# Layer 3 of a four-layer kernel: the expert units move from four bursts into the slots of the recurrence

## The reference

```python
# s: delta rule in chunks of 32 tokens, 4 heads of 32 channels
def step(S, inp):
    q_i, k_i, u_i, w_i = inp
    attn = jnp.where(causal, q_i @ k_i.T, 0.0)
    u_adj = u_i - w_i @ S
    o_i = q_i @ S + attn @ u_adj
    return (S + k_i.T @ u_adj, o_i)
# then s = rmsnorm(gated mix of o_i, three FIR filters and v) @ Wo.T
# f: mixture of experts, 8 experts, 2 per token, capacity 1280 tokens each
hid = einsum('ech,ehf->ecf', inp, W_in);  a, g = split(hid, 2)
out_e = einsum('ecf,efh->ech', gelu(a) * g, W_out)   # then gathered back and weighted
```

## Time and profile before

| what | value |
|---|---|
| the profiled execution's own time | 3312.5 us |
| its span, first to last instruction | 3310.7 us |
| mean granted TensorE clock, share of 2.4 GHz | 0.882 |
| TensorE matmul busy | 2952.2 us, 89% |
| VectorE, ScalarE, GpSimd busy | 56%, 40%, 43% |
| first burst to the end | from 2617 us on |

### The profile page before, as it was taken

How to read it: one execution, slowest core, us unless ns; L and a number is a source line. 1 busy time by engine, 2 the same in 40 slices (tenths; PEclk the granted TensorE clock), 3 DMA queues, 4 the chain that set the end, 5 groups by cost and what they waited for, 6 DMA issues and landing times.

```text
span 3310.7 us, 38793 instructions
## 1 busy us (share of the span) xinstructions
PE 2952.2 (89%) x13864; PEld 1823.9 (55%) x13864; DVE 1841.8 (56%) x3075; ACT 1314.4 (40%) x3221; POOL 1429.1 (43%) x1348
## 2 busy tenths in 40 slices
PE   7896799999999998799999999999789788888876
PEld 3564355555555555355555554444478666666765
DVE  6868577677777766465655554444433534343313
ACT  4453433443443343345555555444412342413201
POOL 3324366676676776267777775000013200101144
PEclk8997899999999999799999999998777775857666
DMA  5451100000000000600000000221022111111111
GB/s 183 151 181 53 50 1 1 1 1 1 1 1 1 1 1 1 145 17 14 1 1 1 1 1 20 74 74 64 30 64 87 43 28 37 31 40 39 34 39 45
DMA packets 160928, 128.88 MB, mean 39 GB/s; under 512 B 97688, under 2 KB 136864, under 8 KB 160224
## 3 DMA queue, kind: packets, MB, share of 16 engines
q1 hardware_dynamic: 148832, 90.13, 9.7%
q0 software_dynamic: 11904, 36.27, 3.4%
HBM read 105.70 MB, written 38.47 MB: 44 GB/s over the span
## 4 chain that ended last, share of the span: by engine, by line
PE 49%; DVE 4%; ACT 3%; issue 2%; another core or an unknown queue 1%; SPq 0%; POOL 0%; DMA 0%; DVEq 0%; ACTq 0%
PE bank L63 44%; PE bank L2051 4%; DVE work L3178 1%; DVE work L3180 1%; SPq L3198 0%; DVE work L3137 0%; ACT L3105 0%; PE bank L2749 0%; DVE weights_even L3137 0%; DVE work L1984 0%; DVE work L3294 0%; POOL weights_odd L2814 0%; PE bank L2904 0%; ACT work L3106 0%
## 5 line engine op out<-in xcount | busy, mean ns | idle before, releaser
L63 PE MATMUL bank<-work 64*128 64x256 f32 (+5 forms) x4384 | 654.3, 365 | 28.1 <-DVE work L3294 7.9
L1491 POOL TENSOR_TENSOR work<-work 128x512 f32<-128x512 f32 x384 | 494.9, 1289 | 320.4 <-DVE work L1483 303.4
L63 PEld LDWEIGHTS bank<-work 64*128 64x128 f32 (+4 forms) x4384 | 468.3, 185 | 260.2 <-issue 137.3
L2039 POOL TENSOR_SCALAR work<-work 128x256 f32<-128x256 f32 x512 | 465.0, 926 | 240.9 <-DVE work L2030 240.8
L63 PE MATMUL bank<-weights_odd,normed_channels 128*128 128x512 f32 (+3 forms) x1152 | 527.9, 566 | 22.4 <-DVE work L1483 15.4
L63 PE MATMUL bank<-work,weights_even 128*32 128x128 f32 (+4 forms) x1136 | 344.9, 482 | 50.0 <-DVE work L1010 15.7
L2024 ACT ACTIVATE work<-bank,work 128x256 f32<-128x256 f32 x512 | 235.9, 473 | 195.0 <-DVE work L2010 190.9
L1483 DVE TENSOR_TENSOR work<-bank,work 128x512 f32<-128x512 f32 x360 | 245.5, 686 | 110.0 <-PE bank L63 106.5
L63 PEld LDWEIGHTS bank<-weights_odd,normed_channels 128*128 128x128 f32 x1152 | 186.6, 199 | 161.5 <-issue 83.1
L63 PEld LDWEIGHTS bank<-work,weights_even 128*32 128x32 f32 (+4 forms) x1136 | 162.2, 193 | 194.4 <-issue 136.4
L2783 POOL TENSOR_TENSOR weights_odd<-weights_odd 128x512 f32<-128x512 f32 x40 | 50.7, 1267 | 491.6 <-ACT weights_odd L2778 491.6
(11 more groups left out here) (307 smaller groups left out, 4535.4 us busy)
## 6 DMA issues: line engine op xcount, KB each, us to landing
work<-gate_rows_L SPq DMA_DIRECT2D x64, 256.0 KB, 3.1
filter_matrices<-in_L_filters SPq DMA_DIRECT2D x24, 512.0 KB, 8.1
work<-filter_matrices SPq DMA_DIRECT2D x16, 768.0 KB, 4.2
expert_rows_in<-in_zeros SPq DMA_DIRECT2D x8, 640.0 KB, 11.3
weights_odd<-expert_rows_in SPq DMA_DIRECT2D x40, 128.0 KB
expert_rows_out<-weights_odd SPq DMA_DIRECT2D x40, 128.0 KB
weights_even<-expert_rows_in SPq DMA_DIRECT2D x20, 128.0 KB
expert_rows_out<-weights_even SPq DMA_DIRECT2D x20, 128.0 KB
```

What stands on the lines that cost most here:

```text
L63: return pe.matmul(out, lhsT, rhs, start=first, stop=last, skip_group_check=True)
L1491: gp.tensor_tensor(self.sum_of(p), self.sum_of(p), self.product_of(p), ALU.add).then_inc(s["l1_add"], 1)
L2039: gp.tensor_scalar(p[:, c], p[:, c], self.sums(n, half, i), None, ALU.mult).then_inc(s["l2_p"], 1)
```

## The change

The bursts go. Quarter 0 gets 14 units, quarters 1 and 2 get 13 each, quarter 3 none. Unit n of a quarter has its place in slot 5 + 3n, its up one slot later and its down in the slot where the next unit is placed. The first seven units of a quarter use banks 2 (a, y) and 7 (x, g), which uw leaves free and the heads take later; the others use banks 0 and 1, after the front is done. The waits follow: heads 0 and 1 wait for unit 6's y and g copies, the next front for the last unit. GpSimd takes all 40 in one loop. On SyncE the grams, results, weights and loads are issued slot by slot, and `sync_inverses` stands at slot 37. The mix loads the table for Ln and Exp right after Square.

```diff
+L3_UNITS_OF = (14, 13, 13, 0)
+L3_UNIT_SLOT, L3_UNIT_STEP, L3_FIRST_SET = 5, 3, 7
+def unit_due(q, slot, lag):
+    n = event(slot, L3_UNIT_SLOT, L3_UNIT_STEP, lag, L3_UNITS_OF[q])
+    return None if n is None else sum(L3_UNITS_OF[:q]) + n
-        self.b_stage, self.b_x, self.b_y, self.b_a, self.b_g = b[7], b[4], b[3], (b[0], b[2]), (b[1], b[7])
+        self.b_stage, self.b_ya, self.b_xg = b[7], (b[2], b[0]), (b[7], b[1])
-    def tensor_burst(self, pe, on, quarter):
...
+    def tensor_units(self, pe, on, quarter, slot):
+        if (n := unit_due(quarter, slot, 3)) is not None:
+            self.tensor_down(pe, on, n)
+        if (n := unit_due(quarter, slot, 0)) is not None:
+            self.tensor_place(pe, on, quarter, n)
+        if (n := unit_due(quarter, slot, 1)) is not None:
+            self.tensor_up(pe, on, n)
...
+            elif L3_UNITS_OF[quarter] > 0:
+                self.moe_done(on, "moe_act", MOE_ACT, (("y", "second")[n], last_unit(quarter, 0)))
...
             a.activation(x, cols(self.sum, g), ACT.Square).then_inc(done, 1)
+            a.preload_act_table_set(EXP_AND_LN)
             self.done(on, "l3_mix_mm", MIX_MM, g, "mean")
...
         for quarter in range(QUARTERS):
-            self.tensor_burst(pe, on, quarter)
             for slot in range(L3_PERIOD + self.TAIL * (quarter == QUARTERS - 1)):
...
                 elif (g := self.join_due(slot, 1)) is not None:
                     self.tensor_join(pe, on, g)
+                self.tensor_units(pe, on, quarter, slot)
...
+        for quarter in range(QUARTERS - 1):
+            self.sync_triangles(sp, on, quarter + 1)
+            for slot in range(L3_PERIOD):
+                for n, step in self.front_steps(quarter, slot):
+                    if step >= 6 and (g := self.front_of(n, 1)) is not None:
+                        self.sync_gram(sp, on, g, step - 6)
+                if (n := unit_due(quarter, slot, 3)) is not None:
+                    self.sync_result(sp, on, n)
+                    e, last = divmod(n + 1, L3_PER_EXPERT)
+                    if last == 0 and e + 1 < EXPERTS:
+                        self.sync_weights(sp, on, e + 1)
+                if (n := unit_due(quarter, slot, 0)) is not None and n + 3 < L3_UNITS:
+                    self.sync_place(sp, on, n + 3)
+                if slot == self.INVERTED:
+                    self.sync_inverses(sp, on, quarter + 1)
+    INVERTED = 37
```

More of the change, by code:

```diff
@@ L2318, with unit_set, last_unit @@
 MIX_DVE = ("gate", "sum", "unit")
-MOE_STEPS = tuple((q, t) for q in range(QUARTERS) for t in range(L3_BURST + 3))
-def unit_due(q, t, lag):
-    return q * L3_BURST + t - lag if 0 <= t - lag < L3_BURST else None
+def unit_due(q, slot, lag):
+    n = event(slot, L3_UNIT_SLOT, L3_UNIT_STEP, lag, L3_UNITS_OF[q])
+    return None if n is None else sum(L3_UNITS_OF[:q]) + n
+def unit_set(n):
+    q = next(q for q in range(QUARTERS) if n < sum(L3_UNITS_OF[:q + 1]))
+    return int(n - sum(L3_UNITS_OF[:q]) >= L3_FIRST_SET)
+def last_unit(q, which):
+    return sum(L3_UNITS_OF[:q]) + (L3_FIRST_SET if which == 0 else L3_UNITS_OF[q]) - 1
 def events(parts):
-    return tuple((what, unit_due(q, t, lag)) for q, t in MOE_STEPS for what, lag in parts if unit_due(q, t, lag) is not None)
+    return tuple((what, unit_due(q, slot, lag)) for q in range(QUARTERS) for slot in range(L3_PERIOD) for what, lag in parts
+                 if unit_due(q, slot, lag) is not None)
 BY_GROUP = lambda what: tuple((what, g) for g in range(GROUPS))
-MOE_MM = BY_GROUP("stage") + events((("x", 0), ("a", 1), ("g", 1), ("y", 3))) + BY_GROUP("join")
-MOE_ACT = BY_GROUP("stage") + events((("x", 0), ("gelu", 1), ("second", 1), ("y", 3))) + BY_GROUP("silu")
+MOE_MM = BY_GROUP("stage") + events((("y", 3), ("x", 0), ("a", 1), ("g", 1))) + BY_GROUP("join")
+MOE_ACT = BY_GROUP("stage") + events((("y", 3), ("x", 0), ("gelu", 1), ("second", 1))) + BY_GROUP("silu")
 MOE_POOL = events((("gated", 1),)) + BY_GROUP("scale")
@@ L3210, in tensor_uw @@
             on.wait_ge(s["l3_sum_act"], 2 * GROUPS)
+            self.moe_done(on, "moe_act", MOE_ACT, ("stage", GROUPS - 1))
         else:
@@ L3510, in scalar @@
                     self.scalar_silu(a, on, g)
+                self.scalar_units(a, on, quarter, slot)
     def vector(self, v, on):
@@ L3571, in gpsimd @@
         next(setup)
-        for quarter in range(QUARTERS):
-            self.gpsimd_burst(gp, on, quarter)
+        for n in range(L3_UNITS):
+            self.gpsimd_gated(gp, on, n)
         for g in range(GROUPS + 2):
```

80 lines of the change are left out of this document (31 added, 49 removed).

## The result

The changed kernel takes 3260.69 us in the median of four runs (3257.80 to 3272.97); the kernel before, beside it, takes 3305.99 (3295.89 to 3312.02). The ratio is 0.9873, with an interval of 0.9836 to 0.9911: 1.3% faster, 45.3 us. The prediction said 3273, faster, with a range from 3220 to 3332.

A forecast was written before the change was run, and what follows sets the result against it. TensorE, busy 89% of the span, was taken as the bound, its clock deciding the sign. Terms -129.8 + 9 + 35 + 40 + 13 - 2.5 + 6 gave about -29 us off 3302.5: 3273 us, range 3220 to 3332.

The forecast's parts named there:

- rival 2: Recurrence clock stays at 0.67 to 0.78 and units pay the half price: +45, 3347 us, slower; chance 0.20 with what lies toward it.
- The recurrence: Slots 4 to 27, 8 units per quarter: four fifths of work at full clock, +35 us, 1.5 per unit.
- The heads: Slots 28 to 36, 3 units per quarter, no idle time to give: net 4.4 us per unit, +40.
- A unit here starts at 5.9: Heads: a unit costs 5.9 us, the half-clock price, before any gain from raising the clock.
- One in two, for some 3.4 us: Heads: one up in two raises the clock for some 3.4 us, saving about 1.5 us per unit.
- Rival 1: Full clock everywhere, heads and mix too: about -142, 3160 us, half the way 3217; chance 0.08 in full or half.
- The mix: Slots 37 to 47, 3, 2 and 2 units: 28.1, 24.2, 24.2 us against 21.4, called +13.
- A Gelu has two slots until its down, 5 us or more: Quarters 0 to 2: Gelu table loads of 1.28 us, some four per period, are covered and cost nothing.
- some 1.5 of the waits stays: Mix, busy 12.4 of 21.4 us before: with units in it, only some 1.5 us of TensorE's waits remain.
- SyncE's queue: Unit results stand behind 32 inverse DMAs from slot 37 on: 2 us of wait per period, +6, bounds 0 and 24.
- Rival 3: SyncE's queue becomes the wait, 8 us per period instead of 2: +18, 3291 us; chance 0.20 together with rival 4.
- Rival 4: Nothing hidden, each unit lengthens its period by 2.84 us: -9, 3293 us; chance 0.20 together with rival 3.

The follow-up runs named there:

- thin units: Changed kernel with each unit's up and down matmuls cut to three of 32 columns, all waits, copies, products and DMAs kept; 3260.15 us in one run.

## Why the prediction was right

**Removal and sign.** The bursts went as a whole and nothing else in their place: -129.8. The clock decided, as said: rival 2, which had the recurrence at 0.78 or below, is excluded by 0.89 to 0.91, and thin units show the half of it that is true: without dense matmuls the clock of two of the three recurrences is 0.64 and 0.66 (0.84 in the third).

**The recurrence, right.** Predicted 78, 79 and 64 us; measured 77.4, 81.0 and 65.9. Per unit 1.6 against 1.5. The clock came as assumed; two smaller misses nearly cancel, by luck: the pauses left are 7.6, 9.6 and 8.4 us where 5, 6.5 and 5 were put, and the busy time is 1.3 to 3.1 us shorter. The timeline of TensorE in the first of them, changed kernel: transposes, gram, up, w and o, all at full clock in the order assumed.

```profile
2685.73 0.38 PE L2748 MATMUL bank<-constants,weights_odd 128*128 128x128 f32 x2
2686.04 1.15 PE L63 MATMUL bank<-work,weights_even 32*128 32x128 f32 x8
2687.62 1.89 PE L63 MATMUL bank<-weights_odd 128*128 128x256 f32 x8
2689.44 1.06 PE L63 MATMUL bank<-work 128*32 128x128 f32 x8
2690.34 1.04 PE L63 MATMUL bank<-work,weights_even 128*32 128x128 f32 x8
```

**The heads, mis-sized by half.** 4.4 us a unit predicted, 2.3 measured (20.5 over nine). The step that failed is "A unit here starts at 5.9", which has the stage begin at half clock. The recurrence hands over its full clock, and the first 10 to 11 us of each heads stage still run at it; the first up there takes 1.97 us each time. After that the clock falls, and "One in two, for some 3.4 us" was near the mark: of the three ups that ran at half clock, the one in the first period (2753.95) was followed by 3 us at full clock, the two others by none. The heads of the first and of the second period in the changed kernel:

```profile
2740.93 1.97 PE L63 MATMUL bank<-weights_odd 128*128 128x256 f32 x8
2742.83 1.15 PE L63 MATMUL bank<-weights_even 32*128 32x128 f32 x8
...
2918.81 3.76 PE L63 MATMUL bank<-weights_odd 128*128 128x256 f32 x8
2922.51 7.76 PE L63 MATMUL bank<-work 32*128 32x128 f32 x32
```

The first up of a stage takes 1.97 us, a later one 3.76, with 32 small records behind it in 7.76. Rival 1, the clock up everywhere, had a third of its way here: 0.73, 0.65 and 0.64 where it wanted 1.00. The Trainium skill, TensorE: Matmul & The Clock Gate, section Why this matters for your kernels, advises to keep TensorE continuously busy for the full clock. The heads of the changed kernel have at most 1.7 us without matmul in 34 and are still at 0.64 to 0.73, so here too the trace agrees only in part.

**The mix, mis-sized the other way.** The step that failed is "A Gelu has two slots until its down, 5 us or more". Between the up and the down of a mix's last unit (of its last two in the first mix) the two slots hold no other matmul, so TensorE waits for the whole of the unit's chain, 3.55 us with the table load and 2.12 without. With it goes "some 1.5 of the waits stays". The units there cost 22.8 us, 3.3 each, against 13 plus 6 for a stall. The clock was better than assumed (0.88), but the time without matmul is 11.2, 8.7 and 8.6 us, where it was 9.0 before and 1.5 were to stay. Most of the old waits were filled, as meant. One of TensorE's waits for VectorE in a mix of the kernel before, and the same matmul in the changed one:

```profile
2789.26 2.07 PE L63 MATMUL bank<-work,weights_odd 128*128 128x512 f32 x2 [2.23 <-DVE work L3378]
```

```profile
2778.60 1.02 PE L63 MATMUL bank<-work,weights_odd 128*128 128x512 f32 x2
```

Of the 9.0 us, 3.0 are left (for Square and the mix's own copy). New ones took their place, 8.2, 5.7 and 5.6 us, all of them for the units' own steps: 5.6, 3.5 and 3.6 for GpSimd's product, the rest for the copies. Table loads are a part of that: without the Gelu's the mixes are 5.5 us shorter, though the three periods only 1, and without the preload 18.6 longer. Thin units, whose three mixes are only 1.6 us shorter, show that it is the unit's chain and not its matmuls; taking two units away (-12) shows the place.

**SyncE's queue, +6 predicted, 0 measured.** TensorE and ScalarE wait for no result. The inverse DMAs' issue (from 2936.78, 15.0 us) ends ahead of the next uw by 10 us, for the longer mix gives it time. Rival 3 did not occur. Rival 4, nothing hidden at 2.84 a unit, would be 3293 us; the recurrence's 1.6 is below it, and thin units show that its sum of parts is wrong in kind: TensorE's price for a unit can't be added without what it does to the clock.

**uw and the last period.** Three uw cost 4.5, where four were put at 9 because each would start at half clock. Only the first did (7.04 us for its first u); the others took 5.42, 3.77 and 3.92, behind mixes whose units had the clock up. With one unit in two slots, where the mixes have no unit, it is 6.9 each time. The last period is 8.6 us shorter, 2.5 of it the preload. The other 6 were not foreseen, and their cause stays open: nothing else is edited there but the start, and TensorE does the same work in 103.1 us in place of 111.3, at a clock of 0.68 in place of 0.63. The period takes 140 to 157 us in eight executions with units in the slots and the joins left alone, and 159.2 and 157.1 in the two with bursts.

From -29 to -54.7 lead the heads (-19.5), uw (-4.5), start and last period (-8.4), the recurrence (+3.2) and mix with SyncE's queue (+3.8). By the medians the change won 45.3 us where 29.5 were forecast. The prediction stood above the median of the runs by 12.3 us, 0.4%, and not by the 15.8 between the two gains, because the kernel before also came out 3.5 us slower than the median it started from. That it stood so close is in part luck: heads and mix were both mis-sized, in opposite directions.

## What to carry to other kernels

- On this kernel, dense matmuls over the whole array that are interleaved with small ones cost less than their own time, since they hold the clock for the small ones (seen in two of three recurrences); judge such a move by the granted clock of the stage that takes them in, and take the matmuls away once to see it (here: 86 us of them removed, nothing won).
- Put hidden work where the receiving stage has both time and free queues: a unit cost 1.6 us in the recurrence, 2.3 in the heads, 3.3 in the mix and nothing in the wait ahead of the first uw, as long as two of them fit (a third put uw off by 4.3 us); at one unit in two slots in place of three the recurrence took 5.7 for each more.
- A table preload that measures as nothing may be what the next change lives on: look at it again whenever two users of different tables become neighbours in ScalarE's order.

## What had not been expected of the hardware

- Lighter work was slower work: the first recurrence has 69.8 us of TensorE busy time with whole units and 76.5 with thin ones, at a clock of 0.91 and 0.64; the second 71.4 and 74.8, at 0.89 and 0.66.
- The third recurrence with the same thin units kept 0.84. What decides between the two outcomes in stages so alike was not found.
- Behind five matmuls of 512 columns and a pause of 1.8 to 2.1 us the next join took 2.02 us (five times in two kernels); behind the same five and a pause of 2.4 to 3.45 us it took 3.5 to 3.8 (three times).
